# Where a batch's attended values are turned and projected: from the batch change and heads 0 and 1 into heads 0 and 1 and heads 2 and 3

## The reference

```python
o1 = _attn(q, k1, v1, causal[None, None])
o2 = _attn(q, ks, vs)
o3 = _attn(q, kw, vw, winmask[None, None])
g = gate[:, :, None, None, None]
o = g[:, 0] * o1 + g[:, 1] * o2 + g[:, 2] * o3
o = o.transpose(0, 2, 1, 3).reshape(B, T, N_HEAD * VDIM)
return o @ Wproj          # and then h = h + this
```

## Time and profile before

| what | value |
|---|---|
| median of the runs | 1754.34 us (1753.4 to 1754.41) |
| profiled execution | 1754.28 us, its span 1752.5 us |
| PE busy | 1365.7 us (78%) |
| DVE busy | 1399.5 us (80%) |
| ACT busy | 1209.9 us (69%) |
| POOL busy | 1362.3 us (78%) |
| mean granted clock of PE | 0.964 |

### The profile page before, as it was taken

How to read it: one execution, slowest core, us unless ns; L and a number is a source line. 1 busy time by engine, 2 the same in 40 slices (tenths; PEclk the granted TensorE clock), 3 DMA queues, 4 the chain that set the end, 5 groups by cost and what they waited for, 6 DMA issues and landing times.

```text
span 1752.5 us, 61262 instructions
## 1 busy us (share of the span) xinstructions
PE 1365.7 (78%) x19368; PEld 1140.4 (65%) x19368; DVE 1399.5 (80%) x4989; ACT 1209.9 (69%) x3280; POOL 1362.3 (78%) x1680
## 2 busy tenths in 40 slices
PE   1042388889888988888888888888888888888788
PEld 0021277777777777777777777777777777777643
DVE  4756678888888888878887888878888888888835
ACT  0032178877787788778887788778877887777634
POOL 6775578977897789779987898789877997899510
PEclk9986599999999999999999999999999999999989
DMA  5110133223332323232233233332333332333200
GB/s 99 23 26 6 30 73 54 54 48 69 56 64 48 66 55 61 55 67 55 54 57 63 53 64 55 59 55 54 55 62 52 64 58 42 64 66 69 57 4 22
DMA packets 327657, 93.59 MB, mean 53 GB/s; under 512 B 321104, under 2 KB 323024, under 8 KB 327520
## 3 DMA queue, kind: packets, MB, share of 16 engines
q1 hardware_dynamic: 324448, 88.61, 27.2%
q0 software_dynamic: 3072, 3.15, 1.1%
HBM read 6.64 MB, written 1.05 MB: 4 GB/s over the span
## 4 chain that ended last, share of the span: by engine, by line
POOL 51%; issue 23%; DVE 10%; PE 9%; DMA 3%; POOLq 2%; ACT 2%; DVEq 0%; ACTq 0%; SPq 0%
POOL big L438 9%; POOL big L437 8%; POOL big L398 6%; POOL qk L440 5%; POOL qk L441 5%; POOL vh L492 4%; POOL kparts L469 4%; POOL qparts L458 4%; DVE S L1029 3%; POOL osum L485 2%; PE S L1377 2%; DMA kh<-kparts 2%; POOL o_b L487 2%; DVE big L1039 1%; POOL kparts L472 1%
## 5 line engine op out<-in xcount | busy, mean ns | idle before, releaser
L653 ACT ACTIVATE big<-S,negm 128x128 f32<-128x128 f32 (+3 forms) x1536 | 575.6, 448 | 196.2 <-DVE negm L1029 195.6
L1039 DVE SCALAR_TENSOR_TENSOR big<-PT,big 128x384 f16<-128x384 f32 (+3 forms) x1024 | 471.3, 499 | 17.1 <-ACT big L665 11.4
L665 ACT ACTIVATE big<-PT 128x384 f16<-128x384 f32 (+3 forms) x1024 | 417.3, 458 | 90.1 <-PE PT L1402 67.6
L1029 DVE CUSTOM_DVE_ANT_0 S<-S,mask_c,unscale 128x128 f32<-128x128 f32 (+3 forms) x512 | 284.7, 556 | 160.9 <-PE S L1377 157.3
L1377 PE MATMUL S<-k1T,qh 128*128 128x128 f16 (+3 forms) x1536 | 294.9, 301 | 141.0 <-DMA qh<-qparts 101.3
L1377 PE MATMUL S<-kh,qh 128*128 128x128 f16 (+1 forms) x3072 | 320.0, 241 | 0.0
L1424 PEld LDWEIGHTS O<-vh,big 128*128 128x128 f16 x8064 | 273.7, 96 | 22.9 <-issue 6.3
L1424 PE MATMUL O<-vh,big 128*128 128x33 f16 x8064 | 283.1, 178 | 4.4 <-issue 3.9
L437 POOL TENSOR_TENSOR big<-qk,cst 128x576 f32<-128x576 f32 (+2 forms) x144 | 182.5, 1267 | 104.9 <-ACT qk L594 103.1
L1377 PEld LDWEIGHTS S<-kh,qh 128*128 128x128 f16 x3072 | 227.3, 99 | 55.2
L1409 PE MATMUL PT<-cst,big 128*128 128x128 f32 x1408 | 244.5, 278 | 2.7 <-DVE big L1039 2.6
(11 more groups left out here) (296 smaller groups left out, 2092.0 us busy)
## 6 DMA issues: line engine op xcount, KB each, us to landing
lat_b<-lat_all SPq DMA_DIRECT2D x8, 448.0 KB, 3.1
qh<-qparts SPq DMA_TRANSPOSE x128, 3.1
kh<-kparts SPq DMA_TRANSPOSE x128, 3.5
xnT_all<-xnT_b SPq DMA_DIRECT2D x14, 128.0 KB, 2.5
xn_b<-xn_all SPq DMA_DIRECT2D x8, 128.0 KB, 2.8
xnT_b<-xnT_all SPq DMA_DIRECT2D x8, 128.0 KB, 2.7
out_dram<-h_all SPq DMA_DIRECT2D x8, 128.0 KB, 2.0
xn_all<-xn_b SPq DMA_DIRECT2D x7, 128.0 KB, 2.0
```

What stands on the lines that cost most here:

```text
L653: last = nc.scalar.activation(pr[par][:, lo:lo + n], S[par][:, lo:lo + n], ACT.Exp, bias=negm[par][:, k:k + 1], scale=-1.0)
L665: last = nc.scalar.activation(pT[par][:, 0, lo:lo + n], PT[:, lo:lo + n], ACT.Copy, scale=PSCALE)
L1029: last = v.tensor_tensor_reduce(out=z, in0=z, in1=m, scale=unscale[:] if k == 0 else kfix[:], scalar=3.0e38, op0=ALU.add, op1=ALU.min, acc ...
L1039: v.scalar_tensor_tensor(pT[par][:, 1, lo:lo + n], PT[:, lo:lo + n], PSCALE, pT[par][:, 0, lo:lo + n], ALU.mult, ALU.subtract).then_inc(s[ ...
```

## The change

The sixteen transpositions of a batch's `o_b` leave `behind`. They go to heads 0 and 1 of the next batch (steps 1 and 2 of each, one chunk of four blocks per step) and write bank X, where the output projection stood; ACT copies the even chunk behind its `take_hi` of step 1, DVE the odd one behind its maxima of step 2, and PE waits for ACT before the odd chunk and for DVE before the key projection of step 3. The output projection and DVE's addition go, with their steps unchanged, to heads 2 and 3. POOL may write `o_b` for the new batch only when it is turned, so from the second batch on each `branch_sum` waits for `oT_psum` in front of its second addition. More heads are written out instead of looped: heads 0 to 3 on PE and DVE (0 and 1 before), heads 0 and 1 on ACT (none before).

```diff
--- before.py
+++ after.py
@@ branch_sum (POOL)
                 g.wait_ge(s["osum_part"], b * NH + hh + 1)
+                if b > 0:
+                    g.nop(nofuse=True)
+                    g.wait_ge(s["oT_psum"], b * 4)
+                    g.nop(nofuse=True)
                 g.tensor_tensor(o_b[:, :, ds(hh * VD, VD)], osum[:], obr[par][:, :, 2, :], ALU.add).then_inc(s["osum_done"], 1)
@@ turn (ACT)
                     if last < 2 or t < 3:
                         take_hi(u + 1, (t + 1) % NT, U + t + 1, rows)
+                    if back is not None and t == 1:
+                        act.wait_ge(s["oT_psum"], back * 4 + 2 * p + 1)
+                        copy(oT[:, 2 * p, :], X[:, 0:512]).then_inc(s["oT_act"], 1)
@@ behind (ACT)
                 copy(vh[0][:, 0, :, 0:VD], vall[:, :, 0:VD]).then_inc(s["v_high"], 1)
-                if not first:
-                    attended(0)
                 probs(0, 0, b, U)
                 lead(LEAD.index("kp2"), nxt, b * NH)
-                if not first:
-                    attended(2)
                 probs(1, 1, b, U + 1)
@@ turn (DVE)
-                    if back is not None and t == 2:
+                    if back is not None and t == 2 and early:
+                        dve.wait_ge(s["oT_psum"], back * 4 + 2 * p + 2)
+                        v.tensor_copy(oT[:, 2 * p + 1, :], X[:, 0:512]).then_inc(s["oT_dve"], 1)
+                    if back is not None and t == 2 and not early:
                         half_residual(back, p)
@@ behind (DVE)
                 value(b, 7)
-                if not first:
-                    attended(b - 1, 1)
                 maxima(0, 0, U)
-                if not first:
-                    attended(b - 1, 3)
                 maxima(1, 1, U + 1)
@@ TensorE
+            def attended_rows(b, c, x):
+
+                if c == 0:
+                    pe.wait_ge(s["osum_done"], (b + 1) * NH + 2)
+                if c % 2 == 0:
+                    x_wait(x)
+                if c % 2 == 1:
+                    pe.wait_ge(s["oT_act"], b * 2 + c // 2 + 1)
+                for t in range(NT):
+                    last = tp(X[:, t * P:(t + 1) * P], o_b[:, t, c * P:(c + 1) * P], ident)
+                last.then_inc(s["oT_psum"], 1)
+
@@ turn (PE)
-                    if back is not None and t in (1, 2):
+                    if back is not None and early and t in (1, 2):
+                        attended_rows(back, p * 2 + t - 1, xb + 1)
+                    if back is not None and early and t == 3:
+                        pe.wait_ge(s["oT_dve"], back * 2 + p + 1)
+                    if back is not None and not early and t in (1, 2):
                         project_rows(back, p * 2 + t - 1, xb + 1)
-                    if back is not None and t == 3:
+                    if back is not None and not early and t == 3:
                         pe.wait_ge(s["h_done"], back * 2 + p + 1)
@@ behind (PE)
-                if not first:
-                    pe.wait_ge(s["osum_done"], H + 2)
-                    pe.wait_ge(s["pT_sb"], 2 * H * NT + 2)
-                    attended(0)
-                    attended(1)
                 pe.wait_ge(s["v_act"], b * 5 + 5)
...
                 scores(0, 0, 0, H * NT)
                 lead("kp2", b, nxt)
-                if not first:
-                    attended(2)
-                    attended(3)
                 scores(1, 1, 0, H * NT + 1)
                 scores(2, 2, 0, H * NT + 2)
-                if not first:
-                    pe.wait_ge(s["oT_act"], b * 2)
-                    pe.wait_ge(s["oT_dve"], b * 2)
                 turn_probs(0, 0, H * NT)
@@ heads (PE; DVE alike, ACT with heads 0 and 1)
-                for p in range(2):
-                    turn(p, b * NH + p, xbase(b) + p * 2, p, 0, rows=0 if rows and p == 1 else None, back=b - 1 if b > 0 else None)
-                with pe.Fori(1, NH // 2 - 2) as hp:
+                for h in range(4):
+                    turn(h, b * NH + h, xbase(b) + h * 2, h % 2, 0, rows=h // 2 if rows and h % 2 == 1 else None,
+                         back=b - 1 if b > 0 else None, early=h < 2)
+                with pe.Fori(2, NH // 2 - 2) as hp:
```

More of the change, by code:

```diff
@@ L674, in take_hi, with turn @@
                     last.then_inc(s["pT_hi"], 1)
-            def turn(b, h, xb, p, last, nxt=None, rows=None, more=True):
+            def turn(b, h, xb, p, last, nxt=None, rows=None, more=True, back=None):
                 H = b * NH + h
@@ L729, in behind @@
             def behind(b, nxt, U, first):
-                def attended(c):
-                    act.wait_ge(s["oT_psum"], (b - 1) * 4 + c + 1)
-                    copy(oT[:, c, :], PT[:, 0:512]).then_inc(s["oT_act"], 1)
                 value(b, 6)
@@ L756, in heads @@
             def heads(b, rows=False):
-                with act.Fori(0, NH // 2 - 2) as hp:
+                for p in range(2):
+                    turn(b, p, xbase(b) + p * 2, p, 0, rows=0 if rows and p == 1 else None, back=b - 1 if b > 0 else None)
+                with act.Fori(1, NH // 2 - 2) as hp:
                     for p in range(2):
@@ L1128, in half_residual, with turn @@
                 v.tensor_tensor(hb, X[:, i * 2 * C:(i + 1) * 2 * C], hb, ALU.add).then_inc(s["h_done"], 1)
-            def turn(b, H, p, last, nxt=None, rows=None, back=None):
+            def turn(b, H, p, last, nxt=None, rows=None, back=None, early=False):
                 U = H * NT
@@ L1194, in heads @@
             def heads(b, rows=False):
-                for p in range(2):
-                    turn(b, b * NH + p, p, 0, rows=0 if rows and p == 0 else None, back=b - 1 if b > 0 else None)
-                with dve.Fori(1, NH // 2 - 1) as hp:
+                for h in range(4):
+                    turn(b, b * NH + h, h % 2, 0, rows=h // 2 if rows and h % 2 == 0 else None,
+                         back=b - 1 if b > 0 else None, early=h < 2)
+                with dve.Fori(2, NH // 2 - 1) as hp:
                     turn(b, b * NH + hp * 2, 0, 0, rows=hp if rows else None)
@@ L1439, in project_rows, with turn @@
                     last.then_inc(s["attn_psum"], 1)
-            def turn(h, H, xb, p, last, b=None, nxt=None, rows=None, back=None, more=True):
+            def turn(h, H, xb, p, last, b=None, nxt=None, rows=None, back=None, early=False, more=True):
                 U = H * NT
```

## The result

| | kernel before | changed kernel |
|---|---|---|
| median of the runs | 1754.34 us | 1787.55 us (1785.18 to 1793.96) |
| profiled execution, its span | 1754.28, 1752.5 us | 1793.96, 1792.2 us |
| mean granted clock of PE | 0.964 | 0.953 |

The ratio is 1.0197, 95% interval 1.0162 to 1.0231: the change makes the kernel 33 us slower. The forecast was 1776 (1756 to 1792): right in sign, inside the range, 11.5 us too low. The profiled execution is the slowest of the four, 6 us above the median, so its pieces add up to more than 33. Some executions of several kernels, the kernel before among them, ran with a lower mean clock and took 1788 us or more (one of experiment 10 took 2182); all medians and ratios here leave them out, and the traces of experiments 2, 8 and 11 are of such executions and are not read.

What follows compares the result with a forecast made beforehand. PE and the engines feeding it were taken to set the pace in the edited stretch, POOL later. Heads 27.3, POOL's wait 1.3, old clock cases -10.1 and new falls 3.3 sum to 21.8 on 1754.3: 1776 us, range 1756 to 1792.

Steps and rivals of the forecast that it cites:

- The batch change gives 0: At seven batch changes, scores start earlier but PE then waits for head 1's key DMA: 0, at best 11 us gained.
- Heads 0 and 1, +2.4 a batch: PE waits for ACT's bank copies and DVE copies more: head 1 ends 2.4 us late; bounds 0 to 3.5.
- Heads 2 and 3, +1.3 and +0.2: Each head receives two projections of 1.08 us: head 2 lengthens by 1.3 us, head 3 by 0.2.
- The wait on POOL, +1.3: Second wait before POOL's second addition, 112 times at 0.1 us, shows only in the last batch: +1.3 us, bounds 0 and 11.
- New clock falls in head 0, +3.3: PE's new 2.0 us idle in head 0 drops its clock in a third of seven batches: +3.3 us, bounds 0 and 9.8.
- Slow-clock cases of head 3 gone, -10.1: Projections fill PE's idle time in head 3, so its slow-clock cases vanish: -10.1 us, bounds -12 and 0.
- rival 3: Clock falls at each boundary and the old slow cases stay, moved to heads 4 and 5: +38 us, 1793 us; chance 0.16.
- the last batch: PE's shift by head 4 exceeds what POOL has to spare in the last batch: +3.9 us, bounds 1 and 4.

Runs made afterwards that it cites:

- experiment 10: Kernel before with ten unused transpositions in step 1 of every odd head from 3 to 13: 1753.62 us, ratio 0.9990.
- experiment 2: Kernel before with heads 0 to 3 written out on PE and DVE, 0 and 1 on ACT, all work where it was: 1760.08 us, ratio 1.0017.
- 8: Kernel before, transpositions kept at the batch change, output projection one token block in step 1 of each of heads 2 to 5: 1751.9 us, ratio 0.9989.
- experiment 11: Changed kernel with both copies first, one projection block a head in heads 2 to 5, unused transpositions in head 0 and odd heads: 1753.4 us, ratio 0.9989.
- Experiments 5 to 7: Changed kernel with ACT's copy ahead of its take_hi (5), DVE's ahead of its maxima (6), both (7): 1779.16, 1778.97, 1765.04 us.
- Experiment 3: Kernel before with the output projection in written-out heads 2 and 3, transpositions still between the batches: 1769.49 us, ratio 1.0068.
- Experiment 4: Changed kernel with chunk 0 transposed four times over, 12 superfluous transpositions a batch in head 0: 1784.24 us, ratio 1.0158.
- experiment 1: Kernel before with only the second wait and its two no-ops before POOL's second addition, from the second batch on: 1759.1 us, ratio 1.0013.
- 9: Changed kernel with both copies first and one projection block in step 1 of each of heads 2 to 5: 1766.41 us, ratio 1.0071.

## Why the prediction was right in sign and 11 us short

- **The batch change gives 0.** Right. PE scores at 398.77 as computed, and the key DMA gates the same place (408.29 for 408.6). The wait there was 1.61 us, not 2.0, mostly because the scores could begin 0.3 us earlier than before.
- **Heads 0 and 1, +2.4 a batch.** Right in size: in batch 4, whose clock stays full, batch change and both heads take 15.0 + 14.3 + 12.1 = 41.4 us against 16.4 + 11.7 + 11.1 = 39.2, +2.2. Experiments 5 to 7 show the cause, the copies standing behind other work: with both copies first, 3.7 us of it go, and the two heads are as short as before the change.
- **Heads 2 and 3, +1.3 and +0.2.** Right: 11.1 and 11.1 in undisturbed batches. Experiment 3 has them alone.
- **The wait on POOL, +1.3.** 0.117 us each for 0.1, and 2.3 us in the runs, from nothing to 5. Within its bounds.
- **New clock falls in head 0, +3.3: mis-sized.** The step says "I take a third of seven". It was five of seven. The price of 1.4 us was about right for four of them (0.5, 1.4, 1.2 and 1.3 us above 14.3); the fifth, batch 6, took 4.3 us because its key DMA landed late as well. Together 8.7 us. Experiment 4 takes the falls away, and in its trace 8.5 us of these heads with them; in the runs that gain is not clear of their spread.
- **Slow-clock cases of head 3 gone, -10.1: the step that failed.** They did leave head 3: its six pieces are 68.5 us against 75.2, though each was to grow by 0.2 us. But the step took them "as gone", and head 5 has them: six pieces of 77.8 us, 63.6 before, +14.1; head 3 and head 5 together are a loss of 7.4 us where 10.1 were to be gained. The bound "0, if they move to head 4 or 5" was the truth, and rival 3, which said that and named 1793 us, lies 5.5 us above the measurement where the forecast lies 11.5 below. A filled head 3 doesn't remove a wait that arises behind it. So the number lies inside the range because the range reached towards rival 3, and not because this term held.
- **The sum of the pieces**, profiled against profiled: 6 x 2.2 for the batch change and heads 0 and 1, 8.7 for the clock there, 6 x 1.3 for head 2, -6.7 for head 3, +14.1 for head 5, and +4.3 for the last batch (154.3 us against 150.0; 3.9 predicted) make 41.4, for 39.7 in the spans (the stretches left out of this sum make up the rest); 6 of these are the distance of this execution from the median.

Where do these cases sit? In the kernel before and in experiment 1 (heads 2 on looped) in head 3. With four heads written out and the projection in heads 2 and 3 (the changed kernel, experiments 3 to 7) in head 5. With six written out and the projection in heads 2 to 5 (9) mostly in heads 6 and 7, and some in 3 and 4. In all of these the written-out heads end where the projection ends, so their traces can't tell which of the two the cases follow. In the runs the written-out heads alone cost 3 us (experiment 2), and the projection moved as well 12 (experiment 3). In the trace PE waits in them for a DMA that lands late, of the queries or of the keys ahead of them. The DMA that turns the queries, in head 5 of batches 1 and 5 of the changed kernel (a case and none), last number the us from issue to landing:

```profile
qh<-qparts SPq DMA_TRANSPOSE x1, 4.7
```

```profile
qh<-qparts SPq DMA_TRANSPOSE x1, 3.1
```

The wait behind the first is 3.54 us at 468.49. In batches 2, 4 and 6 the DMA of the keys just ahead of it is late (4.1, 4.0 and 5.2 us from issue to landing, 3.6 as a rule). Why they land late there stays open, and with it whether the loops, the projection or something else decides it.

## What to carry to other kernels

When a copy empties the one bank that two pieces of work share, put it first on its engine, in the time in which the producer waits anyway; here two copies of 0.6 and 0.7 us, behind 0.9 us of other work, cost 1.3% of the kernel. Before you count a stall as gone because work now fills its head, ask what makes the awaited thing late: here the stall came back two heads later. And price an idle time of TensorE with the clock behind it; if it can't be avoided, unused transpositions in it can pay (experiment 11 against 9; not clearly in 4 and 10).

## What the runs showed of the hardware

- The granted clock fell from 1.00 to 0.50 (2.4 to 1.2 GHz) around waits of only 1.38 to 1.84 us in head 0 of batches 1, 2, 3 and 5, and stayed there for 3 to 7 us, while in batches 4 and 7 of the same trace it stayed at 1.00 behind waits of 1.85 and 1.89 us. So the length of the wait alone doesn't tell whether the clock falls. The waits of batch 3 (a fall) and of batch 4 (none), and a window behind the first:

```profile
779.84 0.34 PE L1378 MATMUL S<-k1T,qh 128*128 128x128 f16 x3 [1.38 <-DMA kh<-kparts]
...
966.59 0.34 PE L1378 MATMUL S<-k1T,qh 128*128 128x128 f16 x3 [1.85 <-DMA kh<-kparts]
```

```profile
780.30:787.00 6.70, 6.00 (x45) 5.45 (x43) 3.13 (x13) 2.84 (x8) 5.83 (x8) 0.50 0.42 91
```

- The longest case is head 0 of batch 6, where the key DMA landed after 5.2 us for the usual 3.4; the clock was at 0.50 for some 10 us. Its start from the timeline, and windows of it 4 us later (0.50 is the granted clock):

```profile
1338.06 0.50 PE L1378 MATMUL S<-k1T,qh 128*128 128x128 f16 x3 [3.97 <-DMA kh<-kparts]
```

```profile
1342.00:1344.00 2.00, 2.00 (x13) 1.63 (x12) 0.00 (x0) 0.66 (x3) 0.71 (x1) 0.50 1.01 188
1344.00:1346.00 2.00, 2.00 (x22) 1.94 (x21) 1.53 (x7) 0.68 (x2) 0.00 (x0) 0.50 0.23 44
```

- Work that nobody needs made a kernel faster: 12 transpositions in head 0 and ten in the odd heads by 0.8% (11 against 9). The 12 alone held the clock of head 0 at 1.00 in all of batches 1 to 6 (experiment 4).
- The same DMA at the same place of the program lands at different times: that of the keys in head 0 of the changed kernel after 3.4 us in five batches, 3.6 in one and 5.2 in one, that of the queries in head 5 after 3.1 to 4.7.
